# The sum over sixteen attention heads: one strided reduction, or four contiguous additions

## The reference

```
q, k, v = layernorm(x) Wq', ctx Wk', ctx Wv'      16 heads of 8
attn    = softmax(q k' / sqrt(8), axis=1)         axis 1 is the HEAD axis
x       = x + (attn v) Wo'
y       = layernorm(x)
x       = x + y + shared experts(y) + routed top-2 experts(y)
```

## Time and profile before

| | |
|---|---|
| median of 3 runs | 599.83 us (597.85 to 602.25) |
| span of the profiled execution | 516.6 us |
| its own time | not listed beside the span; the runs' median less the span is 83.2 us |
| busy: TensorE, VectorE, ScalarE, GpSimd | 383.5, 368.1, 291.5, 278.2 us |
| sum over the heads (L855) | 16 of 3.706 us, 59.3 us, from 84.3 us on |
| weight preparation and q, k, v | up to 73 us |
| attention | 73 to about 217 us |
| router, shared experts, routed experts, gathering | from there to the end |

### The profile page before, as it was taken

One profiled execution on the slowest core, in us unless ns is written; L12 is line 12 of the kernel. 1 busy time (PEld: TensorE's weight loads), 2 busy tenths in 40 slices (PEclk: granted clock), 3 DMA queues, 4 the chain that ended last, 5 costly groups with the idle time before them and its releaser, 6 DMA issues.

```text
span 516.6 us, 11703 instructions
## 1 busy us (share of the span) xinstructions
PE 383.5 (74%) x3844; PEld 306.4 (59%) x3845; DVE 368.1 (71%) x663; ACT 291.5 (56%) x525; POOL 278.2 (54%) x276
## 2 busy tenths in 40 slices
PE   5457754988688698685899879949979797979600
PEld 2223322877577687583566557637969696869500
DVE  4947775889999999969948786734747464646437
ACT  3764423434567575534678568925746464646446
POOL 7392001664576667650776777631757475656700
PEclk9967885889999899797899899987999898999955
DMA  8900000000000000000111123122322222221089
GB/s 228 394 14 2 0 0 0 1 1 1 1 1 1 0 2 1 0 1 2 42 52 39 52 82 104 32 58 58 87 63 81 71 63 68 66 75 53 23 213 275
DMA packets 36234, 29.82 MB, mean 58 GB/s; under 512 B 4181, under 2 KB 33496, under 8 KB 35809
## 3 DMA queue, kind: packets, MB, share of 16 engines
q1 hardware_dynamic: 31648, 20.84, 14.0%
q0 software_dynamic: 4544, 8.44, 5.0%
HBM read 17.55 MB, written 12.62 MB: 58 GB/s over the span
## 4 chain that ended last, share of the span: by engine, by line
PE 29%; DVE 7%; issue 7%; POOL 3%; DMA 2%; ACT 1%; SPq 1%; POOLq 0%; DVEq 0%
PE banks L1440 3%; PE banks L1455 3%; PE banks L1441 3%; PE banks L1442 3%; PE banks L1454 3%; PE banks L1456 3%; POOL results L456 2%; PE banks L1422 2%; DVE E L919 2%; PE banks L1372 2%; PE banks L1376 1%; PE banks L1374 1%; PE banks L1356 1%; PE banks L1357 1%; PE banks L1358 1%
## 5 line engine op out<-in xcount | busy, mean ns | idle before, releaser
L377 POOL TENSOR_TENSOR E<-E,rZ 128x1024 f32<-128x1024 f32 x32 | 75.2, 2371 | 89.5 <-DVE rZ L858 89.5
L456 POOL DMA_INDIRECT results<-vPad,qRep x78 | 84.8, 1087 | 65.8 <-DVE vPad L1127 43.0
L446 POOL DMA_INDIRECT gathered<-xs,slot x64 | 69.5, 1085 | 42.5 <-DVE xs L1000 18.9
L1135 DVE TENSOR_TENSOR E<-kRep,E 128x512 f16<-128x512 f32 x78 | 54.2, 694 | 41.9 <-ACT E L689 41.9
L687 ACT ACTIVATE kRep<-banks 128x512 f32<-128x512 f32 x78 | 46.8, 600 | 64.8 <-PE banks L1442 48.8
L1263 PE MATMUL banks<-E,vPad 128*128 128x128 f32 x512 | 70.1, 296 | 12.5 <-POOL E L377 12.5
L1263 PEld LDWEIGHTS banks<-E,vPad 128*128 128x128 f32 x512 | 67.5, 210 | 17.1 <-issue 8.8
L575 ACT ACTIVATE E<-banks 128x1024 f32<-128x1024 f32 x32 | 31.0, 1021 | 57.3 <-PE banks L1256 57.3
L855 DVE TENSOR_REDUCE Z<-E 128x128 f32<-128x2048 f32 x16 | 59.3, 3706 | 0.0
L1454 PE MATMUL banks<-wprojL,E 128*128 x312 | 57.5, 223 | 0.9 <-DVE E L1135 0.9
L919 DVE TENSOR_TENSOR E<-kRep,E 128x512 f16<-128x512 f32 x64 | 45.9, 732 | 16.1 <-ACT E L650 15.5
(11 more groups left out here) (203 smaller groups left out, 931.0 us busy)
## 6 DMA issues: line engine op xcount, KB each, us to landing
qRep<-gathered SPq DMA_DIRECT2D x39, 129.0 KB, 2.2
qRep<-results SPq DMA_DIRECT2D x16, 256.0 KB, 5.2
E<-in_wfc_t SPq DMA_DIRECT2D x1, 2560.0 KB, 9.5
X<-in_x SPq DMA_DIRECT2D x4, 512.0 KB, 7.2
out<-X SPq DMA_DIRECT2D x8, 256.0 KB, 3.9
xs<-in_wproj_t SPq DMA_DIRECT2D x1, 1280.0 KB, 12.2
results<-vPad,qRep POOLq DMA_INDIRECT x78, 2.5
gathered<-kPad SPq DMA_DIRECT2D x9, 129.0 KB
```

The lines of the kernel that those rows point to most:

```text
L377: g.tensor_tensor(heads, heads, rZ[:, k % 2, :].unsqueeze(1).broadcast_to([P, HH, P]), ALU.mult).then_inc(attn_ready, 1)
L446: g.indirect_dma_start(out=gathered, out_offset=bass.IndirectOffsetOnAxis(ap=slot[:, k, i:i + 1], axis=0), in_=xs[:, i, :], in_offset=None ...
L456: g.indirect_dma_start(out=results, out_offset=bass.IndirectOffsetOnAxis(ap=xg[:, k, h, 2 * D:ROW].bitcast(I32), axis=0), in_=yg[:, k, h, ...
```

## The change

The single reduction over a strided view becomes four additions. The first adds heads 8 to 15 to heads 0 to 7, eight whole tiles at once, into a buffer of 4 KB a partition; the next two halve that in place, from eight tiles to four to two; the last adds the remaining two tiles into `Z`. Each waits on a new semaphore, `z_step`, for the one before. The buffer `head_sums` is laid over the last eight tiles of `xs`. The reciprocal and everything else stay as they are.

```diff
--- before.py
+++ after.py
@@ -159,6 +159,10 @@
         stats1 = E_flat[:, NE * F:NE * F + TILES * 6].rearrange("p (t s) -> p t s", s=6)
         xs_flat = xs[:].rearrange("p t r -> p (t r)")
 
+
+        head_sums = xs_flat[:, (TILES - 2 * TP) * ROW:(TILES - 2 * TP) * ROW + 2 * HH * P].bitcast(F32).rearrange(
+            "p (h q) -> p h q", h=HH)
+
         select = xs_flat[:, 0:2 * 2 * QUARTER * P].rearrange(
             "p (w l g m) -> p w l g m", w=2, l=2, g=QUARTER)
         wq, wk, wv = (xs_flat[:, 2048 + 2 * D * i:2048 + 2 * D * i + 2 * D].bitcast(F32)
@@ -212,8 +216,8 @@
         kPad_ready, vPad_ready = sem("kPad_ready"), sem("vPad_ready")
 
         raw_ready, max_ready, s_ready = sem("raw_ready"), sem("max_ready"), sem("s_ready")
-        exp_done, z_ready, rz_ready, attn_ready = (
-            sem(n) for n in ("exp_done", "z_ready", "rz_ready", "attn_ready"))
+        exp_done, z_step, z_ready, rz_ready, attn_ready = (
+            sem(n) for n in ("exp_done", "z_step", "z_ready", "rz_ready", "attn_ready"))
         o_ready, oT_ready, y_ready, x_added = (sem(n) for n in ("o_ready", "oT_ready", "y_ready", "x_added"))
 
         xn2_ready, x2_added, t2_ready, hi_ready, lo_ready, x2_ready = (
@@ -852,8 +856,13 @@
 
             def sum_heads(u, k):
                 dve.wait_ge(exp_done, 2 * u + 2)
-                v.tensor_reduce(Z[:, k % 2, :], E[:, k].rearrange("p h q -> p q h"), AX_X,
-                                ALU.add).then_inc(z_ready, 1)
+                v.tensor_tensor(head_sums[:, 0:HH], E[:, k, 0:HH], E[:, k, HH:H], ALU.add).then_inc(z_step, 1)
+                dve.wait_ge(z_step, 3 * u + 1)
+                v.tensor_tensor(head_sums[:, 0:4], head_sums[:, 0:4], head_sums[:, 4:8], ALU.add).then_inc(z_step, 1)
+                dve.wait_ge(z_step, 3 * u + 2)
+                v.tensor_tensor(head_sums[:, 0:2], head_sums[:, 0:2], head_sums[:, 2:4], ALU.add).then_inc(z_step, 1)
+                dve.wait_ge(z_step, 3 * u + 3)
+                v.tensor_tensor(Z[:, k % 2, :], head_sums[:, 0], head_sums[:, 1], ALU.add).then_inc(z_ready, 1)
                 dve.wait_ge(z_ready, u + 1)
                 v.reciprocal(rZ[:, k % 2, :], Z[:, k % 2, :]).then_inc(rz_ready, 1)
```

## The result

The changed kernel takes 603.48 us (median of 20 runs, 598.05 to 606.52) where the kernel before takes 599.3 us (20 runs beside it). The ratio is 1.0074, interval 1.0049 to 1.0099: plus 4.4 us, 2.9 to 5.9. Forecast was plus 5, 605 us, with 0.50 on a change within one per cent. The profiled execution took 604.1 us, with a span of 602.3. All medians here are taken over all runs, while ratios leave out runs more than 1.5% above the fastest of their kernel, which makes a difference of note for one version alone (last_strided, four of its 12 runs).

What follows compares the result with a forecast made beforehand. VectorE's loop was taken to set the pace. The 15 turns gave plus 6.7 us, the first sum minus 1.0, possible short turns 0.8 off; taken as plus 5 on 599.8: 605 us, range 598 to 610.

Steps and rivals of the forecast that it cites:

- The saving without the wait: Four additions take 2.75 us where the reduction took 3.75: 1.0 us less per unit, 16 us in all, if unhindered.
- seed turns: Three attention turns with the deviation's seed, sums starting after GpSimd's multiplications: 35.1 us before, 32.7 forecast.
- The exclusion: VectorE additions with two SBUF inputs and GpSimd's multiplications lock each other out of a shared port for full instructions.
- the seven plain turns: Attention turns without seed or GpSimd subtraction, excluding the last: 8.3 us each, 58.1 in all, 56.7 before.
- the four with the subtraction: Turns with GpSimd's subtraction of a pair right behind its multiplications: 9.1 us each, 36.5 in all, 32.1 before.
- short turns: Turns where the first addition slips between GpSimd's halves, 0.3 us shorter; five or six possible, half counted, 0.8 us.
- The 83 us around the span: The 83.2 us between the profile's 516.6 us span and the 599.83 us median were put around the span.
- the same stall: The 8-element half_var, taking 2.27 us and ending with GpSimd's multiplication, was held to wait as the two-input additions do.
- Rival 1: No exclusion for these f32 additions, all 16 sums take 2.75 us: minus 12 us, 588; chance 0.14.
- Rival 2: GpSimd keeps the port across back-to-back instructions, between its halves and before the subtraction: plus 7 us, 607; chance 0.12.
- Rival 3: The additions do not beat the reduction, since the hop is not what costs: plus 9 us or so; chance 0.03.
- Rival 4: The exclusion costs only part where additions overlap a multiplication's end: 597 to 602 us; chance 0.09.

Runs made afterwards that it cites:

- last_strided: The changed kernel with the strided reduction put back for the last sum alone (unit 15): 601.34 us, ratio 1.0016 to the kernel before.
- hybrid: The kernel before with the four additions only for units 0, 6, 10 and 14, the strided reduction for the other twelve: 509.82 us, ratio 0.9918.
- pairs: The kernel before with E laid out so that each two heads are neighbours, still one reduction: 583.57 us, ratio 0.9757.
- pair with doubled writes: Kernel before and changed kernel, GpSimd's multiplications replaced by zeros written twice without reading SBUF: 506.45 us (ratio 0.9876) and 503.09 us (0.9791).
- after_fill: The changed kernel with GpSimd writing zeros once, reading nothing, in place of its multiplications: 484.06 us, ratio 0.9410 to the kernel before.
- before_fill: The kernel before with GpSimd writing zeros once, reading nothing, in place of its multiplications: 498.7 us, ratio 0.9706.
- after_again: The changed kernel, unchanged, measured again beside the kernel before in the second job: 603.89 us, ratio 1.0102.
- after_third: The changed kernel, unchanged, measured once more beside the kernel before in the third job: 517.73 us, ratio 1.0094.

## Why the prediction was right

**The bound.** VectorE's loop set the pace and still does: in the changed kernel it is busy 83.6 of 87 us between 131 and 218 us. About 16.5 of these are waits for GpSimd inside the additions (19.3 and 16.2 us for ten of each, at 1.21 and 0.69 alone), so the busy share by itself does not prove it. Two versions that shorten the sum without a wait do: hybrid gains all of the 4.0 us that it takes off VectorE, pairs 15.8 us in the stage of 21.5, up to where TensorE binds.

**The saving without the wait.** Forecast 2.75 us from the start of the sum to the reciprocal; measured 2.75 at the seed turns and 2.76 at the first sum. The four sizes came out at 1.21, 0.69, 0.42 and 0.29 us.

**The exclusion.** Read from the two subtractions of the earlier trace rows, and right for f32 additions: they alternate with GpSimd's multiplications instruction by instruction. The forecast ending "1.09 after GpSimd" is 1.07 to 1.09 in the trace. The pair with doubled writes shows that an addition waits for the subtraction, which reads SBUF (1.50 us for 0.69), and not for a write (1.22 us, eight times). The Trainium skill, page "SBUF — State Buffer", section "SBUF: two separate sides", has it so: two SBUF inputs on VectorE clash only with a GpSimd instruction that reads SBUF.

**Turn by turn**, from forecast to measured: the seven plain turns 58.1 to 57.7 us; the four with the subtraction 36.5 to 36.5; the three with the seed 32.7 to 32.2; the last 8.2 to 8.04; the stage plus 5.6 us, forecast 6.7 less the 0.8 that I took off for short turns, 5.9. The first sum minus 0.9. Sum plus 4.7, in time plus 4.4. The closeness is in part luck: of the 1.1 us by which the turns stayed under their sum, short turns made only 0.5, and the seed turns, where nothing had been taken off, another 0.5.

**What was mis-sized.** Three plain turns (8.13, 8.14, 8.13 us) and the last took the short way between the halves; I had allowed for five or six. In the other four plain turns (8.30 to 8.33) the first addition was asked for 3.87 to 4.78 us after the reciprocal, past the gap near 3.37: in three of them VectorE had waited 1.42, 1.62 and 0.44 us for TensorE before the maximum, in one it had the statistics of a pair. In the seed turns I took 0.2 a turn for the small GpSimd operations; VectorE lost nothing (1.21 and 0.69), GpSimd's operations did the waiting (1.06 and 0.65 for 0.20 in all three).

**What was wrong.** The 83 us around the span. They were no part of the execution that left the trace: with the 1.7 to 2.2 us of the other runs it took about 518.5 us, an estimate, and so was one of the short kind, while the median of 599.83 was of the long kind. The prediction did not reckon with two kinds. Its 605 stands because the shift is made in the attention, which is the same in both; that it is, the later runs showed. Wrong too was "the same stall" for the 8-element `half_var`: it waits for a mere write as well, which the additions do not.

**The rivals.** Rival 1 (no exclusion, 588) is refuted by the waits of the first two additions in the trace after, and after_fill shows roughly what was lost to the exclusion (minus 14.6 us without it). Rival 2 (GpSimd keeps the port): VectorE got in at both boundaries, 102.85 between the halves and ahead of the subtraction at 148.81. Rival 3: the additions do beat the reduction where free. Rival 4: the waits are full ones; an addition of 1.21 us ends 1.07 to 1.09 us after the GpSimd instruction that it waited for.

## What to carry to other kernels

Before a one-input instruction on VectorE becomes one with two SBUF inputs, look what GpSimd runs at that moment: the saving of 1.0 us a unit here was paid for with waits of up to 2.0 us, in instructions that only look long. One input is not by itself a safeguard, as `half_var` shows: with the small operations beside it, it cost the kernel before some 7 us (three seed turns, 35.1 us there and 27.7 in before_fill). A strided reduction need not be replaced by additions: putting two of the summed values side by side brought it from 3.71 to 2.28 us, with no wait for GpSimd. And when VectorE gets faster, count GpSimd's small operations next, because in the pair with doubled writes they stood in the way as soon as the waits were gone.

## What the runs showed of the hardware

GpSimd's multiplication got faster with the paired layout, 2.14 us instead of 2.36 (medians) for the same 1024 elements; its second input, the reciprocal, is then read twice in a row for each query. Why that helps was not tried.

The kernel before took 513 us in two jobs and 598 in another (599.3 beside the changed kernel at first), the spans with it. The second job (598) and the third (513) are on record with the same chip, so it is not the chip alone. Two stage rows of the changed kernel, in the columns of the earlier trace rows with GB/s as the last one, first from the job of 598 us (after_again), then from that of 513 (after_third):

```profile
260.00:340.00 80.00, 40.42 (x355) 24.04 (x354) 19.61 (x42) 27.34 (x48) 39.48 (x40) 0.69 0.11 35
```

```profile
260.00:340.00 80.00, 71.06 (x813) 49.93 (x812) 57.79 (x125) 60.90 (x109) 59.47 (x56) 1.00 0.23 60
```

In the same 80 us TensorE issues 355 instructions in the one and 813 in the other. In parts of the first its instructions come about 0.7 us or more apart with no wait that the profile can name, and VectorE once stands still for 30.4 us. The slow parts lie where GpSimd scatters the rows to DRAM (L450): from 283 to 306 us, without a scatter, TensorE issues 242 instructions, from 313 to 336 us, beside 19 GpSimd instructions of that kind, only 16. In the job of 513 us it issues 211 and 255 in the same windows, beside 16 and 14 of them, so the scatters alone do not explain it. The attention stage is the same in both (134.5 us). What holds the engines there was not tried and stays open; for a comparison it means that a trace and a time are to be taken from the same job.
